# Local attention in a 25-section kernel: per-head norms by streamed sums and a selecting product, another order of transfers, later sine products

## The reference, cut to what matters

```
h = shift_token(x);  q, k, v = split(h @ wqkv, 3)          # 8 heads of 64, 2 x 1024 tokens
q = q / max(norm(q), 1e-12) * qs;   k = k / max(norm(k), 1e-12) * ksc
q = q * cos * scale + rotate_half(q) * sin * scale          # k: the same, divided by scale
attention in windows of 64 tokens, each looking at its own window and the one before
x = x + o @ wo;  then layer norm, a gated MLP, and x = x + h @ w2 + b2
```

## Time and profile before

| what | value |
|---|---|
| runs | 4381.35, 4387.26, 4872.67 us; median 4387.26 us |
| profiled execution, its own time | 4381.53 us |
| its span | 4379.8 us |
| mean granted TensorE clock | 0.918 of full speed |
| PE, DVE, ACT, POOL busy | 88%, 68%, 54%, 29% of the span |
| the two local-attention stages | about 738 to 1170 us and 1640 to 2080 us |

### The profile page before, as it was taken

The page is one execution under the profiler, slowest core; times in us unless marked ns, Lnnn a source line. Parts: engine busy times, 40 slices in busy tenths (PEclk is TensorE's granted clock), DMA queues, the critical chain, the costliest instruction groups (busy, mean ns, idle before and its releaser), DMA issues.

```text
span 4379.8 us, 63073 instructions
## 1 busy us (share of the span) xinstructions
PE 3866.0 (88%) x22574; PEld 1863.3 (43%) x22576; DVE 2956.8 (68%) x7834; ACT 2377.7 (54%) x4077; POOL 1260.1 (29%) x1851
## 2 busy tenths in 40 slices
PE   8899968999889988998886888999998999969999
PEld 5222335555422235555552235555554334433343
DVE  4899665777589967777446984666667863378732
ACT  3477743566447765666446654454543773327732
POOL 1100022333220013333023872111114323433334
PEclk8799978899979998999987998999997999979999
DMA  1100002222020012221000000000001100011000
GB/s 56 25 20 16 15 35 77 58 57 58 18 64 19 16 48 64 57 56 44 6 11 0 0 9 9 9 18 9 18 32 27 29 11 0 32 25 25 15 0 10
DMA packets 57937, 120.47 MB, mean 28 GB/s; under 512 B 17140, under 2 KB 17140, under 8 KB 56344
## 3 DMA queue, kind: packets, MB, share of 16 engines
q1 hardware_dynamic: 56472, 114.87, 9.9%
q10 hardware_dynamic: 1152, 1.57, 0.2%
HBM read 40.88 MB, written 1.05 MB: 10 GB/s over the span
## 4 chain that ended last, share of the span: by engine, by line
PE 54%; DVE 26%; ACT 6%; POOL 5%; issue 5%; SPq 2%; DMA 1%; ACTq 0%; POOLq 0%; DVEq 0%
PE PS L512 31%; DVE SM L1275 7%; PE PS L1185 7%; PE PS L1137 5%; PE PS L2782 3%; DVE AR L516 2%; PE PS L1167 2%; PE PS L539 1%; SPq L2090 1%; POOL SV L609 1%; DVE AR L2582 1%; DVE AR L597 1%; DVE AR L1986 1%; PE PS L2425 1%; DVE TP L1272 1%
## 5 line engine op out<-in xcount | busy, mean ns | idle before, releaser
L512 PE MATMUL PS<-AR,WS 128*128 128x512 f32 (+1 forms) x2112 | 1050.2, 636 | 75.2 <-DVE AR L516 28.7
L1237 ACT ACTIVATE AR<-PS 128x1024 f32<-128x1024 f32 (+3 forms) x896 | 788.8, 931 | 205.3 <-PE PS L1167 201.2
L1275 DVE TENSOR_REDUCE SM<-PS 128x1 f32<-128x512 f32 x1280 | 803.1, 683 | 72.9 <-PE PS L1137 71.6
L519 ACT ACTIVATE AR<-PS 128x512 f32<-128x512 f32 (+6 forms) x568 | 358.4, 635 | 512.1 <-PE PS L512 422.1
L512 PEld LDWEIGHTS PS<-AR,WS 128*128 128x128 f32 (+1 forms) x2112 | 399.1, 200 | 528.1 <-issue 400.1
L1137 PE MATMUL PS<-AR 51*128 51x512 bf16 (+3 forms) x1792 | 508.2, 383 | 62.6 <-DVE SM L1275 15.9
L1185 PE MATMUL PS<-AR 128*32 128x512 f32 (+3 forms) x3584 | 447.2, 571 | 2.5 <-POOL AR L1327 1.9
L1928 ACT ACTIVATE AR<-AR,SM 128x128 f32<-128x128 f32 x512 | 248.0, 486 | 265.1 <-DVE SM L516 262.3
L1137 PEld LDWEIGHTS PS<-AR 51*128 51x128 bf16 x1792 | 133.2, 94 | 598.5 <-DVE SM L1275 404.4
L1167 PE MATMUL PS<-AR 51*128 51x512 bf16 (+3 forms) x1792 | 288.7, 366 | 8.3 <-ACT AR L1237 5.3
L512 PE MATMUL PS<-AR,H 115*115 115x128 bf16 (+3 forms) x912 | 219.1, 314 | 72.8 <-POOL MBT L1319 14.4
(11 more groups left out here) (321 smaller groups left out, 6888.4 us busy)
## 6 DMA issues: line engine op xcount, KB each, us to landing
TP<-RAW SPq DMA_DIRECT2D x512, 64.0 KB, 2.0
AR<-AR SPq DMA_DIRECT2D x720, 32.0 KB
VXT<-AR SPq DMA_DIRECT2D x120, 128.0 KB, 2.4
WS<-wall SPq DMA_DIRECT2D x4, 3654.5 KB, 11.2
WS<-wall SPq DMA_DIRECT2D x8, 902.5 KB, 4.4
WS<-wall SPq DMA_DIRECT2D x2, 3334.5 KB, 10.8
WS<-wall SPq DMA_DIRECT2D x1, 2384.0 KB, 9.1
WS<-wall SPq DMA_DIRECT2D x1, 1543.5 KB, 6.1
```

What stands on the lines that cost most here:

```text
L512: t = e.matmul(o, l, r, start=(n == 0), stop=(n == len(pairs) - 1))
L519: return e.activation(o, i, ACT.Copy, scale=1.0)
L1237: e.activation(pv[:, :, off:512], sv[:, :, off:512], ACT.Exp, scale=scale).then_inc(*F.at_exp.up((s, u, p2)))
L1275: e.tensor_reduce(top, bank(ring(n + g), m), AX.X, ALU.max).then_inc(*F.at_max.up((s, k, i, rr, k0, g)))
```

## The change

Four edits, all within local attention:

1. The squares are summed in two steps. For each half of a group (four items) there is an item "sum" (keys at n = 4, queries at n = 11, second list): four products with a constant of 32 columns (SUM64, two of them used) as the stationary operand and the 512 squares as the moving one, each into its own 32 partitions of one bank. ACT copies the bank into slot(3). Then an item "norm" per half (keys at n = 5, queries at n = 12): four products with the copied sums as the stationary operand and a constant of 8 columns (PICK64) that picks the used rows. The eight per-item norms are gone. ACT's squares into slots 0 to 2 now wait for "sum", into slot 3 for "norm".
2. The root steps come one slot later: n = 6, 7, 8 and 13, 14, 15, and the split of the key roots at n = 9.
3. The sine products on DVE and the additions on POOL go by the list of slot u-3 instead of u-2.
4. On SP, swap(g+1, j) stands ahead of shifted_values(g, j).

```diff
-            ... ("BLK64C", blkc(64)),
+            ... ("SUM64", np.pad(blkc(64), ((0, 0), (0, 30)))), ("PICK64", pick64()),
+def pick64():
+    o = np.zeros((128, 8), np.float32)
+    for r in range(4):
+        for g in range(2):
+            o[32 * r + g, 2 * r + g] = 1
+    return o
 def l1f_dense(slot_):
-                second = [("norm", g, j) for j, at in enumerate((2, 3, 4, 4, 6, 7, 10, 11)) if n == at] + second
+                second = [("norm", g, z) for z, at in ((1, 5), (0, 12)) if n == at]
+                if n == 4:
+                    second += [("sum", g, 1)]
                 if n == 11:
                     first += [("turn", g, 0)]
+                    second += [("sum", g, 0)]
 def l1f_pe
+                        if name == "sum":
+                            w.wait_ge(*F.head_squared.on((s, g, 3 if j else 7)))
+                    if name == "sum":
+                        for r in range(4):
+                            t = e.matmul(bank(k)[32 * r:32 * r + 32, :], C("SUM64"), slot(r), start=True, stop=True)
+                        t.then_inc(*F.head_summed.up((s, g, j)))
+                        free[k] = F.head_sums.on((s, g, j))
                     if name == "norm":
-                        w.wait_ge(*F.head_squared.on((s, g, j)))
+                        w.wait_ge(*F.head_sums.on((s, g, j)))
                         for i in range(4):
-                            n = 32 * z + 8 * i + 2 * r
-                            t = mm(e, bank(4)[:, n:n + 2], (slot(j % 4)[:, ts_(i)], C("BLK64C")))
+                            n = 32 * j + 8 * i
+                            t = mm(e, bank(4)[:, n:n + 8], (slot(3)[:, ts_(i)], C("PICK64")))
 def l1f_act
-                            w.wait_ge(*F.head_norm.on((s, g, j - 4) if j >= 4 else (s, g - 1, j + 4)))
+                            used = F.head_norm if j % 4 == 3 else F.head_summed
+                            w.wait_ge(*used.on((s, g, 1) if j >= 4 else (s, g - 1, 0)))
+                    if name == "sum":
+                        w.wait_ge(*F.head_summed.on((s, g, j)))
+                        copy(e, slot(3), bank(at[x])).then_inc(*F.head_sums.up((s, g, j)))
 def l1f_dve
-                    if name == "norm" and j in (3, 7):
+                    if name == "norm":
-                for name, g, j in l1f_dense(u - 2)[0] if u > -15 else []:
+                for name, g, j in l1f_dense(u - 3)[0] if u > -14 else []:
-                if g < 8 and n in (5, 6, 7):
+                if g < 8 and n in (6, 7, 8):
-                if g < 8 and n in (12, 13, 14):
+                if g < 8 and n in (13, 14, 15):
-                if g < 8 and n == 8:
+                if g < 8 and n == 9:
 def l1f_pool
-                for name, g, j in l1f_dense(u - 2)[0] if u > -15 else []:
+                for name, g, j in l1f_dense(u - 3)[0] if u > -14 else []:
 def l1f_sp
                 for j in range(8):
+                    if g < 7:
+                        swap(g + 1, j)
                     if j < 4:
                         shifted_values(g, j)
-                    if g < 7:
-                        swap(g + 1, j)
```

More of the change, by code:

```diff
@@ L37, in const_arrays @@
     return [("C", eye - np.float32(1 / 128)), ("AVG", np.full((128, 128), 1 / 128, np.float32)),
-            ("ONE", np.ones((128, 128), np.float32)), ("I", eye), ("BLK8", blk(8)), ("BLK8C", blkc(8)), ("BLK64C", blkc(64)),
+            ("ONE", np.ones((128, 128), np.float32)), ("I", eye), ("BLK8", blk(8)), ("BLK8C", blkc(8)), ("SUM64", np.pad(blkc(64), ((0, 0), (0, 30)))), ("PICK64", pick64()),
             ("MHALF", np.full((128, 64), -0.5, np.float32)),
@@ L1795, in dense @@
                         free[k] = F.head_cos.on((s, g, j))
+                    if name == "sum":
[3 more added lines that the diff above has]
+                        free[k] = F.head_sums.on((s, g, j))
                     if name == "norm":
-                        r, z = ITEMS[j]
-                        w.wait_ge(*F.head_squared.on((s, g, j)))
-                        if j % 4 == 0:
-                            w.wait_ge(*free[4])
+                        w.wait_ge(*F.head_sums.on((s, g, j)))
+                        w.wait_ge(*free[4])
                         for i in range(4):
-                            n = 32 * z + 8 * i + 2 * r
-                            t = mm(e, bank(4)[:, n:n + 2], (slot(j % 4)[:, ts_(i)], C("BLK64C")))
+                            n = 32 * j + 8 * i
+                            t = mm(e, bank(4)[:, n:n + 8], (slot(3)[:, ts_(i)], C("PICK64")))
                         t.then_inc(*F.head_norm.up((s, g, j)))
-                        free[4] = F.head_norm_max.on((s, g, z))
+                        free[4] = F.head_norm_max.on((s, g, j))
                     if name == "v":
@@ L2003, in l1f_dve @@
                         stt(e, dst[:, r, g % 2, :], bank(at[item]), W(g)(scale), W(g)(table)[:, cs(g % 2)], ALU.mult, ALU.mult).then_inc(*F.head_cos.up((s, g, j)))
-                    if name == "norm" and j in (3, 7):
-                        z = ITEMS[j][1]
+                    if name == "norm":
+                        z = j
                         rn = RN[:, 64 * (g % 2) + 32 * z:64 * (g % 2) + 32 * z + 32]
-                        w.wait_ge(*F.head_norm.on((s, g, j)))
+                        w.wait_ge(*F.head_norm.on((s, g, z)))
                         e.tensor_scalar(rn, bank(4)[:, 32 * z:32 * z + 32], 1e-24, None, ALU.max).then_inc(*F.head_norm_max.up((s, g, z)))
```

## The result

| | before | changed |
|---|---|---|
| median of four runs | 4385.35 us | 4417.45 us |
| range | 4381.35 to 4872.67 us | 4404.47 to 4419.03 us |
| profiled execution: span, clock | 4379.8 us, 0.918 | 4416.6 us, 0.912 |

Ratio 1.0071, 95% interval [1.0053, 1.0089]: some 31 us slower. The forecast was 4350 us, 35 us faster than the median of before. (One run of before was in a slower state, at 4872.67 us, and the ratio leaves it out.)

A forecast was written before the change was run, and what follows sets the result against it. PE was taken to bound the kernel, though not in every slot. Per group -2.2 - 0.3 + 0.3 = -2.2 us, -31 over seven groups and two stages; first groups -4, prologue +2: -33, giving 4350 us, range 4320 to 4382.

The forecast's parts named there:

- Term A: n = 2 to 4: one sum (1.06 us) replaces the keys' four norm items (3.26 us), gaining 2.2 us per group.
- Term B: n = 5 to 8: one norm item added, 1.6 us of items removed; gain 0.3 us per group, between 0 and 0.8.
- Terms C and D: n = 9 to 15: PE work moved and DVE crowded at n = 9; loss 0.3 us per group, between -1.2 and +1.4.
- The edits on transfers: Edits 3 and 4: sine-product waits nearly vanish, worth about 2 us per stage in the first two groups; SP order gains nothing.
- Rival 3: DVE chain n = 9 to n = 0: crowding makes the kernel slower, +13 us, 4395 us; chance 0.1.
- Rival 4: PE's clock in the two stages: fewer half-clock slots give 4340 us, more falls from idling 4360 us; chance 0.12.

The follow-up runs named there:

- the filler runs: Changed kernel with unread products added on PE at n = 6, 7 and 10: two-column form 4393.9 us, wide form (eight of 256 columns) 4383.36 us.
- short additions: POOL's additions cut to 128 of 512 columns, other sines left out: changed kernel 4352.94 us, kernel before 4347.28 us.
- The sums alone: Kernel before with edits 1 and 2 only (sums, selecting norms, later root steps): 4391.13 us, ratio 1.0021.
- the order without long operations: Kernel before with DVE's root steps and key-root split put ahead of the sine products within the slot: 4365.35 us, ratio 0.9967.
- another schedule: Eight unread bf16 products of 256 columns at n = 6, 7 and 10, in a kernel other than the changed one: 4389.8 us, 25 us slower than without them.

## Why the prediction was wrong

**Term A held.** n = 2 to 4 went from 12.0 to 10.0 us, 2.0 against 2.2 forecast; a sum takes 8 records in 1.06 us at full clock and 1.93 at half, as the side-by-side row had it. The two copies on ACT, counted as nothing, never held up the selecting products.

**Term B failed.** The step was: the root's first step is 1.15 us against 0.18 for a later one, and guess and first step "only change from one side of a score to the other". The length doesn't belong to the first step. It belongs to POOL's addition, which was running beside it in the earlier trace rows too, from 921.99 to 923.26, where the root operation lasted from 922.16 to 923.31:

```profile
921.99 1.27 POOL L2066 TENSOR_TENSOR AR<-AR,TP 128x512 f32<-128x512 f32 x1 [1.62 <-DVE TP L516]
```

I read one engine's timeline at a time. Edits 2 and 3 together put a root step beside an addition at n = 6, where it stands ahead of the cosine product that frees a gate's bank. n = 5 to 8 grew by 1.4 us (19.2 to 20.6) instead of shrinking by 0.3.

**Terms C and D had the right places and a wrong size.** I counted 0.3 us of loss, at most 1.4. n = 9 to 15 grew by 4.2 us (19.4 to 23.6), n = 0 and 1 by 0.8. The crowding at n = 9 to 11 was there as described (wait for the square 0.50 us, against 0.8), but four things came on top: the split of the roots behind an addition (1.13 instead of 0.17 us), with it PE's wait of 1.64 us for the late maximum, the sum and the next product at or near half clock (1.93 and 1.78 against 1.06 and some 1.0), and the half-clock stretches up to n = 15.

**The edits on transfers.** The sine products' waits vanished as forecast and were worth nothing on the path: with edit 3 alone three of the four groups without gates last as long as before, to 0.3 us, and the fourth is the one that had been slow. Edit 3 alone cost 43 us. I priced a wait that goes and a product that moves, and not what the product starts on another engine. The late shifted values of j = 3 were a real wait at n = 7, small (4.7 us in one stage), where I had counted none. With all edits the groups without gates gained 15 us, not the 4 counted; one profile of each kernel doesn't say why.

**The rivals.** Rival 3, the crowded second half, is nearest in place and sign; it had a chance of 0.1 and a price of +13, for want of the additions and the clock. Rival 4 had the clock as a swing of 10 us either way. In fact half-clock time per gated group tripled, and the filler runs show that the clock took part: some 28 us of the changed kernel's time went when PE's waits were filled with wide products. The missing norm items aren't its first cause: edit 3 alone, with all norm items in place, has the most half-clock time. What rival 4 took from the trace, that the fall at n = 5 had followed no idling, led away from it; the falls that cost most now come behind PE's waits at n = 7 and 10.

**What stays open.** Why the 2.8 us of PE work per group that went bring nothing even with short additions (4353 against 4347), and the 20 us of edit 3 that don't hang on them.

The windows of the groups with gates say where the time goes. With short additions on both sides the change keeps its gain at n = 2 to 4 (12.0 to 9.9 us) and breaks even at n = 5 to 8, but n = 9 to 15 grow from 18.6 to 22.0 and n = 0 and 1 by 0.6. PE's waits that are new or longer there sum to 2.9 us per group with gates: at n = 7 0.7 for ACT's gelu and 0.6 for the shifted values, at n = 11 0.7 for DVE's maximum and 0.5 for the square, at n = 13 0.4 for the maximum over the norms. That is the crowded second half of rival 3 and the late shifted values; which of them decides, no run isolates. POOL waits the other way as well: its division (0.61 us) lasts 1.04 us when it starts behind a sine product on DVE, 34 times now and 13 before, with short additions 34 and 12; no run shows whether that costs time.

The sums alone, with hardly a long root operation, are 9 us slower than before; against the kernel before in the order without long operations (4365) they have PE idle 5.8 instead of 3.6 us per group. That fits a wait at PE for DVE that has taken the place of the removed work, but no run isolates it.

## What to carry to other kernels

Before moving an instruction, lay the timelines of the engines beside each other: an operation that lasts six times as long as its neighbours of the same shape is waiting for somebody, and the move decides whether that lies on the path. When work is taken off the busiest engine but its waits stay, look at whether the clock holds; time gained in one slot was given back at half clock in the next. And price an edit that only removes a wait by the slots it fills, not by the wait's row.

## What the runs showed of the hardware

A DVE operation on 128 x 32 values that reads and writes SBUF (0.18 us) started beside a POOL addition ends when the addition ends: 1.14 us beside 1.27 us, 0.33 beside 0.46. So it was with all 28 long root operations of the changed kernel, and all 32 of the one before. DVE's copy of 128x256 values from PSUM takes its usual 0.42 us beside an addition, also where it starts 0.37 us into it (at 854.64 us in the changed kernel, the addition at 854.27). The Trainium skill has this (SBUF — State Buffer, Who interferes with whom: a DVE instruction with two SBUF inputs contends with a GpSimd instruction that reads SBUF, and the later one waits the whole of it), and the trace agrees; I had not weighed it. The split's first operation, a cast with one SBUF input, waits too (1.13 us), which that sentence doesn't cover.

Unread products in PE's waits lowered the half-clock time of a gated group from 11.9 us to 10.2 in one form and 5.9 in the other, and in another schedule, where they also made PE wait 18.9 us, raised it from 6.6 to 8.2.
